# A two-layer attention kernel: new step order for the second layer, attention output normalised on VectorE

## What is computed

```python
# layer 0
x_norm = (x - mu) * rsqrt(var + EPS) * ln_scale + ln_bias
q, k, v = split(x_norm @ w_qkv + b_qkv)              # 8 heads of 16
attn = softmax(einsum('bqhd,bkhd->bhqk', q, k) * scale)
x = x + einsum('bhqk,bkhd->bqhd', attn, v) @ w_out + b_out
# layer 1
tokens = x @ Win + b_in
t = layernorm(tokens)
q, k, v = heads(t @ Wq), heads(t @ Wk), heads(t @ Wv)
pk, pv = pool2d(k), pool2d(v)                        # 64 positions
_, idx = top_k(einsum('bhsd,bhpd->bhsp', q, pk).max(axis=(1, 2)), 16)
attn = softmax(einsum('bhsd,bhkd->bhsk', q, pk[idx]) * scaling)
tokens = tokens + attn @ pv[idx]
ff = gelu(layernorm(tokens) @ Wf1 + bf1) @ Wf2 + bf2
out = (tokens + ff) @ Wout + bout
```

## Time and profile before

| | before |
|---|---|
| median of 3 runs | 921.74 us (920.42 to 923.03) |
| profiled execution | 920.22 us, its span 918.5 us |
| PE busy | 841.7 us, 92% |
| ACT busy | 615.3 us, 67% |
| DVE busy | 511.5 us, 56% |
| POOL busy | 162.5 us, 18% |
| mean granted TensorE clock | 0.961 |

### The profile page before, as it was taken

The page is one execution under the profiler, slowest core; times in us unless marked ns, Lnnn a source line. Parts: engine busy times, 40 slices in busy tenths (PEclk is TensorE's granted clock), DMA queues, the critical chain, the costliest instruction groups (busy, mean ns, idle before and its releaser), DMA issues.

```text
span 918.5 us, 14785 instructions
## 1 busy us (share of the span) xinstructions
PE 841.7 (92%) x5339; PEld 399.8 (44%) x5339; DVE 511.5 (56%) x1543; ACT 615.3 (67%) x699; POOL 162.5 (18%) x198
## 2 busy tenths in 40 slices
PE   8889989999898989999899988989899998899988
PEld 6324334444343433434344433444335343345665
DVE  6423267655577275754676365863666525633564
ACT  4577867587757867678666876578675876774112
POOL 2503041201330031300430022300412001000100
PEclk9799999999999999999999999999999999999979
DMA  3545324222331124322331123421142223000300
GB/s 72 98 74 94 60 47 88 39 35 59 93 64 33 26 48 105 53 36 59 75 65 29 32 59 92 70 36 38 28 89 45 36 59 69 1 1 25 70 0 25
DMA packets 41214, 48.73 MB, mean 53 GB/s; under 512 B 13872, under 2 KB 31920, under 8 KB 41136
## 3 DMA queue, kind: packets, MB, share of 16 engines
q1 hardware_dynamic: 41136, 47.72, 27.1%
HBM read 5.45 MB, written 4.19 MB: 10 GB/s over the span
## 4 chain that ended last, share of the span: by engine, by line
PE 60%; DVE 25%; ACT 8%; issue 3%; SPq 3%; POOL 1%; DMA 0%; DVEq 0%; ACTq 0%; POOLq 0%
PE O L545 17%; PE S L530 11%; ACT Pr L783 7%; DVE hT L1018 4%; PE BC L566 4%; PE BC L558 4%; PE BC L667 3%; PE BC L651 3%; PE A L477 3%; DVE st L893 3%; PE BC L588 2%; PE A L566 2%; PE S L763 2%; PE BC L606 2%; PE BC L659 2%
## 5 line engine op out<-in xcount | busy, mean ns | idle before, releaser
L783 ACT ACTIVATE Pr<-S 128x1024 f32<-128x1024 f32 x512 | 490.5, 1028 | 152.5 <-PE S L530 152.3
L545 PE MATMUL O<-Pr,Va 128*32 128x512 f32 x2048 | 279.3, 618 | 3.8 <-DVE Ot L997 3.8
L530 PE MATMUL S<-Qs,Ks 49*128 49x512 f32 x1024 | 213.3, 467 | 31.5 <-ACT Pr L783 28.8
L530 PEld LDWEIGHTS S<-Qs,Ks 49*128 49x128 f32 x1024 | 86.3, 186 | 160.8 <-ACT Pr L783 129.0
L545 PEld LDWEIGHTS O<-Pr,Va 128*32 128x32 f32 x2048 | 40.8, 108 | 87.3 <-issue 82.1
L383 POOL COPY Va<-v_new 128x256 f32<-128x256 f32 x32 | 12.4, 406 | 337.7 <-PE O L545 321.5
L799 ACT ACTIVATE tT<-BC,cols 128x512 f32<-128x512 f32 x32 | 24.1, 775 | 45.7 <-PE BC L558 45.7
L997 DVE COPY Ot<-O 128x512 f32<-128x512 f32 x32 | 21.9, 685 | 58.0 <-PE O L545 58.0
L1129 DVE TENSOR_SCALAR hT<-BC,cols 128x512 f32<-128x512 f32 x32 | 24.0, 751 | 45.4 <-PE BC L651 43.9
L1068 DVE TENSOR_REDUCE r<-BC 128x1 f32<-128x512 f32 x64 | 41.1, 681 | 12.9 <-PE BC L606 12.9
L1136 DVE TENSOR_TENSOR Y<-BC,out_bias 128x512 f32<-128x512 f32 x16 | 11.1, 691 | 61.5 <-PE BC L667 61.5
(11 more groups left out here) (190 smaller groups left out, 1149.2 us busy)
## 6 DMA issues: line engine op xcount, KB each, us to landing
Qs<-qh SPq DMA_DIRECT2D x128, 64.0 KB, 2.3
Ks<-kh SPq DMA_DIRECT2D x128, 64.0 KB, 2.3
Q1s<-q1h SPq DMA_DIRECT2D x64, 128.0 KB, 2.4
X<-in_x_dram SPq DMA_DIRECT2D x8, 512.0 KB, 4.0
Qs<-ql SPq DMA_DIRECT2D x64, 64.0 KB, 2.3
Ks<-kl SPq DMA_DIRECT2D x64, 64.0 KB, 2.3
Q1s<-q1l SPq DMA_DIRECT2D x32, 128.0 KB, 2.3
out_dram<-Y SPq DMA_DIRECT2D x16, 256.0 KB, 2.3
```

The lines of the kernel that those rows point to most:

```text
L530: mm = pe.matmul(S[:, c, a * HALF:(a + 1) * HALF], Ks[head, j, kb * P:(kb + 1) * P], Qs[head, j, c * HALF:(c + 1) * HALF], start=True, sto ...
L545: mm = pe.matmul(O[r:r + 32, :], Va[:, kb, 2 * j + a, :], Pr[:, s % 2, c, a * HALF:(a + 1) * HALF], start=(kb == 0), stop=(kb == TILES - 1))
L783: act.activation(Pr[:, s % 2, c, :], S[:, c, :], ACT.Exp, scale=SCALE).then_inc(probs_ready, 1)
```

## The change

- The AT_... constants are new. The second layer of an image now covers 46 steps: 32 beside the next image and 14 (`STEPS + s`: T2, FF, GELU, OUT) beside the image after that. TOKX of the next image moves across the border as well (steps 32 and 33), and the layer norm of X is done an image earlier (`first_norm`).
- Bank turns are worked out ahead of time in tables (`a_turns`, `b_turns`) instead of running counts.
- The attention output is no longer copied, turned by TensorE, divided, and turned back. VectorE transposes O in blocks of 32 x 32 into `OT`, divides there, transposes back into `On`, and four DMAs per pair write it into `attnT`.
- `Pr` has three buffers. TensorE adds one weighted sum in each step; that of step 31 stands at the end of its image, ahead of the next image's flag.
- The four matmuls of the sums of squares become one packed group (AT_BOUND, 26); one reduction over 128 rows, one transpose, and `bound` on one row replace four reductions.
- The product of tok2 with Wout is done in the OUT step, tok2T lies in Y, and `that` and `attnT` have tiles of their own.
- SP's list is reordered; in the tail it is: attention of pair 3, the store of image 6, the stack of image 7's queries, its store. The tail interleaves steps 32 to 45 of image 6 with steps 0 to 45 of image 7.

```diff
-AT_LN0, AT_XN, AT_Q, AT_K, AT_V, AT_TOKX = 2, (8, 10), (11, 12), (13, 14), (15, 16), (18, 19)
-AT_BOUND, AT_FLAG = (20, 21, 24, 26), 27
-AT_AT, AT_TOK, AT_T, AT_Q1, AT_PK, AT_SC, AT_RT, AT_RB = 2, 4, 7, 7, 9, (11, 12, 13, 14), 15, 16
-AT_SEL, AT_S2, AT_E2, AT_PT, AT_TOK2, AT_TT2, AT_T2 = 17, 18, 18, 20, 21, 23, 27
-AT_FF, AT_GELU, AT_OUT = (28, 29), 29, (30, 31)
-
+AT_LN0 = 22
+AT_XN, AT_Q, AT_K, AT_V, AT_TOKX = (10, 12), (15, 17), (19, 21), (23, 31), (32, 33)
+AT_BOUND, AT_FLAG = 26, 28
+AT_TOK, AT_T, AT_Q1, AT_PK, AT_SC, AT_RT, AT_RB = 3, 8, 9, 12, (15, 16, 17, 18), 19, 20
+AT_SEL, AT_S2, AT_E2, AT_PT, AT_TOK2, AT_TT2, AT_T2 = 22, 25, 25, 27, 29, 30, 34
+AT_FF, AT_GELU, AT_OUT = (37, 39), 41, (43, 45)
+AFTER_END = 46
 
...
-        Pr = sb("Pr", [P, 2, 2, T])
+        Pr = sb("Pr", [P, 3, 2, T])
...
+            def attn_out(n, j):
+
+                if j == 0 and n > 0:
+                    for h in range(2):
+                        sp.wait_ge(b_drained[h], b_after(n - 1, K_TOK + h))
+                sp.wait_ge(on_ready, PAIRS * n + j + 1)
+                for a in range(2):
+                    for c in range(2):
+                        r, d = 32 * (2 * a + c), HD * (2 * j + a)
+                        sp.dma_start(attnT[d:d + HD, c * HALF:(c + 1) * HALF], On[r:r + HD, j % 2, :]).then_inc(attn_in[j % 2], 16)
...
+            def image(n):
+
+                if n > 0:
+                    attn_out(n - 1, 3)
+                    stack(n, 2)
+                    stack(n, 3)
+                wait_for_flag(sp, n)
...
                     load_x(n + 2)
-                if not first:
+                attn_out(n, 0)
+                if n > 0:
                     stack1(n - 1)
...
+                if n > 1:
+                    store(n - 2)
+                attn_out(n, 1)
+                if n + 1 < IMAGES:
+                    stack(n + 1, 0)
+                attn_out(n, 2)
+                if n + 1 < IMAGES:
+                    stack(n + 1, 1)
+
...
+            attn_out(IMAGES - 1, 3)
+            store(IMAGES - 2)
...
+                if n == 0:
+                    normalise(1)
...
+            def sums_of_squares(bank, filled):
+
+                for i in range(2):
+                    for h in range(2):
+                        r = 32 * (2 * i + h)
+                        mm = pe.matmul(bank[r:r + 32, :], head_mask_b[:, :], squares[:, i, h * HALF:(h + 1) * HALF],
+                                       start=True, stop=True)
+                mm.then_inc(filled, 1)
...
                     scores(n, s, 1)
                     if s > 0:
                         weighted(n, s - 1)
-                    elif not first:
-                        weighted(n - 1, STEPS - 1)
-                    if s == 1 and not first:
-                        turn_o(n - 1, PAIRS - 1, turns)
-                    if s > 1 and s % TILES == 1:
-                        turn_o(n, s // TILES - 1, turns)
-                    if not last:
-                        before_tasks(n + 1, turns, s)
-                    if not first:
-                        after_tasks(n - 1, s, base + 1)
-
-            image(0, 0, first=True)
+                    if n > 0:
+                        before_tasks(n, STEPS + s)
+                    if n + 1 < IMAGES:
+                        before_tasks(n + 1, s)
+                    if n > 1:
+                        after_tasks(n - 2, STEPS + s)
+                    if n > 0:
+                        after_tasks(n - 1, s)
+                weighted(n, STEPS - 1)
+
+            image(0)
 
             pe.wait_ge(weights_in, 16 * WEIGHT_DMAS)
...
+            for s in range(AFTER_END):
                 for _ in range(WARM.get(s, 0)):
 
                     for a in range(2):
                         head = slice(64 * a, 64 * a + MROW + 1)
                         pe.matmul(S[:, 0, a * HALF:(a + 1) * HALF], Ks[head, 0, 0:P], Qs[head, 0, 0:HALF], start=True, stop=True)
-                after_tasks(IMAGES - 1, s, base + PAIRS + 1)
+                after_tasks(IMAGES - 2, STEPS + s)
+                after_tasks(IMAGES - 1, s)
...
+                g = STEPS * n + s
+                act.wait_ge(scores_ready, 2 * g + c + 1)
+                if c == 0 and g > 2:
+
+                    act.wait_ge(pv_done, g - 2)
+                act.activation(Pr[:, g % 3, c, :], S[:, c, :], ACT.Exp, scale=SCALE).then_inc(probs_ready, 1)
...
+                    if s == AT_TT2 and n > 0:
+                        act.wait_ge(out_done, 2 * 16 * n)
...
+            def bound(own, row):
+
+                both = prow[:, 0:P].rearrange("o (i h e) -> o i h e", i=2, h=2)
+                larger = prow[:, P:P + 64].rearrange("o (i e) -> o i e", i=2)
+                step(own, dve.tensor_copy(prow[:, 0:P], row))
+                step(own, dve.tensor_tensor(larger, both[:, :, 0, :], both[:, :, 1, :], ALU.max))
+                step(own, dve.tensor_tensor(prow[:, 192:224], prow[:, P:P + 32], prow[:, P + 32:P + 64], ALU.add))
+                step(own, dve.tensor_reduce(prow[:, 224:225], prow[:, 192:224], AX.X, ALU.max))
+                return dve.tensor_scalar(flag[:, :], prow[:, 224:225], SAFE_SQUARES, None, ALU.is_gt)
...
-            def copy_o(n, j):
-
+            def divide_o(n, j):
+
+                own = own_attention
+                if n > 0 or j > 0:
+                    dve.wait_ge(on_ready, PAIRS * n + j)
                 dve.wait_ge(pv_done, STEPS * n + TILES * (j + 1))
-                dve.tensor_copy(Ot[:, :], O[:, :]).then_inc(o_copied, 1)
-
-            def divide_o(n, j, turns, own):
-
-                drain_a(turns)
-                o = A[:, :].rearrange("p (t a c e) -> p t a c e", t=4, a=2, c=2)
-                r = rden[:, :].rearrange("p (t a c) -> p t a c", t=4, a=2)
-                step(own, dve.reciprocal(rden[:, :].rearrange("p (u o) -> p u o", o=1),
-                                        A[:, :].rearrange("p (u e) -> p u e", e=32)[:, :, HD:HD + 1]))
-                for c in range(2):
-                    ins = dve.tensor_tensor(
-                        attn[:, 4 * c:4 * c + 4, 2 * HD * j:2 * HD * (j + 1)].rearrange("p t (a d) -> p t a d", a=2),
-                        o[:, :, :, c, 0:HD], r[:, :, :, c:c + 1].to_broadcast([P, 4, 2, HD]), ALU.mult)
-                ins.then_inc(a_drained, 1)
+                dve.transpose(OT[:, :, :].rearrange("p q e -> p (q e)"), O[:, :]).then_inc(o_turned, 1)
+                dve.wait_ge(o_turned, PAIRS * n + j + 1)
+                step(own, dve.reciprocal(rden[:, :].unsqueeze(2), OT[:, :, HD:HD + 1]))
+                step(own, dve.tensor_tensor(OT[:, :, 0:HD], OT[:, :, 0:HD], rden[:, :].unsqueeze(2).to_broadcast([P, 16, HD]),
+                                            ALU.mult))
+                if n > 0 or j >= 2:
+                    dve.wait_ge(attn_in[j % 2], 16 * ATTN_DMAS * (PAIRS // 2 * n + j // 2))
+                dve.transpose(On[:, j % 2, :], OT[:, :, :].rearrange("p q e -> p (q e)")).then_inc(on_ready, 1)
...
-                    if s == 0 and not first:
-                        copy_o(n - 1, PAIRS - 1)
                     if s > 0 and s % TILES == 0:
-                        copy_o(n, s // TILES - 1)
-                    if s == 1 and not first:
-                        divide_o(n - 1, PAIRS - 1, turns, own_o)
-                    if s > 1 and s % TILES == 1:
-                        divide_o(n, s // TILES - 1, turns, own_o)
-                    if not last:
-                        before_tasks(n + 1, turns, own_b, s)
-                    if not first:
-                        after_tasks(n - 1, own_a, s)
-                assert last or own_b[2] == BEFORE_STEPS
-                assert first or own_a[2] == AFTER_STEPS
-
-            image(0, 0, first=True)
+                        divide_o(n, s // TILES - 1)
+                    if n > 0:
+                        before_tasks(n, STEPS + s)
+                    if n + 1 < IMAGES:
+                        before_tasks(n + 1, s)
+                    if n > 1:
+                        after_tasks(n - 2, STEPS + s)
+                    if n > 0:
+                        after_tasks(n - 1, s)
+                    if n == 0 and s == 0:
+                        first_norm(1)
+                    if s == AT_LN0 and n + 2 < IMAGES:
+                        first_norm(n + 2)
+                divide_o(n, PAIRS - 1)
```

More of the change, by code:

```diff
@@ L311, in _ @@
                 sp.dma_start(dst, src).then_inc(weights_in, 16)
-            def image(n, base, first=False, last=False, load=True):
-                wait_for_flag(sp, base)
+            def image(n):
[4 more added lines that the diff above has]
+                wait_for_flag(sp, n)
                 sp.sem_inc(sp_passed, 1)
@@ L522, in scores @@
                 before = 2 * STEPS * n + 2 * s + c - 1
[L523 removed]
+                if before > 0:
                     pe.wait_ge(probs_ready, before)
@@ L720, in _, with image @@
                 by_token_first(BC[h], xhT, win_s[:, :], h)
```

(20 more changed lines are left out.)

530 lines of the change are left out of this document (242 added, 288 removed).

## The result

The changed kernel takes 971.71 us (median of 4 runs, 968.29 to 972.49) where the kernel before takes 921.08 on the same chip (4 runs): 1.0548 times as long, 95% interval 1.0505 to 1.0591. The forecast was 945 with a range of 914 to 968, so the time lies 3.7 us outside the range. The direction was right, the size was 27 us short. The profiled execution took 972.3 with a span of 970.6, 26.8 over the 943.8 of the sum.

The account below looks back on a forecast made before the run. TensorE's in-order list was taken to bound the images, with 12% waits for other engines. 918.5 - 8 - 12.6 + 5 x 2.7 + 4.4 + 28 = 943.8, plus 1.7 around the span = 945.5, given as 945; range 914 to 968.

Parts of the forecast that it names:

- (a): Inner image, steps 9 to 11: exponential queued behind GELU, Q1 copies and table loads; TensorE waits plus half clock, 7.7 us.
- (b): Image border: TensorE waits for the last exponential, flag and branch, and TOKX tasks wait for V's drain and divide; 3.0 us.
- (e): Inner image, steps 15 to 18: waits around Q drains, score maxima and the second divide; 1.7 us.
- (c): Inner image, step 22: V's drain and third divide queue behind the layer norm on VectorE, sum 24 waits; 1.8 us.
- (d): Inner image, step 25: exponentials of the softmax of S2 sit ahead of the attention's exponential 26; 2.4 us.
- Image 0: Prologue and image 0: packed bound matmuls, TOKX gone, Q moved past a wait, border added; 8 us saved (5 to 10).
- Tail: After the last exponential: interleaving images 6 and 7 delays turned tokens, query stack and first scores; +28 us (+20 to +34).
- the rival of VectorE as the bound: Block transposes cost twice the copy, lengthening VectorE's waits by 3.5 us per inner image; 963 us, chance 0.13.
- only the first 0.7 holds up: VectorE's attention work, 2.3 us per pair: only the first 0.7 delays the next weighted sum, as the copy did.
- Table switches: Rival: ScalarE's table loads each cost a drain of 1.3 us, two loads in seven places, +18; 963 us, chance 0.03.
- The one that waits overlap: Rival: after (a) VectorE has caught up, so (c) to (e) and the half clock vanish; 902 us, chance 0.14.
- The one that inner images gain the removed work: Rival: inner images each gain 4.1 us, image 7 even, tail grows; about 907 to 925, centre 919, chance 0.11.

Follow-up runs that it names:

- standstill_filled_2: The changed kernel with 8 dummy matmuls ahead of the scores of step 11 in images 2 to 7; 957.34 us, ratio 1.0386.
- only_attention_part: The kernel before with only VectorE's block transposes, division and four DMAs per pair replacing the old attention output path, order untouched; 928.84 us, ratio 1.0053.
- three_repairs: The changed kernel with GELU in step 10, layer norm of X at step 12 (22 in image 0), image 6 finished before image 7 in the tail; 911.96 us.

## Why the prediction was right in direction and wrong in size

Of the 26.8 us missing, 14.4 lie in images 2 to 6, 6.2 in prologue and image 0, 3.6 in the tail, 1.8 in image 1, 1.0 in image 7 (27.0 with rounding).

The steps that failed are three terms of the sum. In an inner image the half clock was put at 1.7 us, behind one standstill only; it was 5.6. The work left on TensorE was put at 88.9; it was 92.0. In image 0 the forecast let a light step make up for a heavy one, which the trace doesn't bear out. The first two make 7.0 us an inner image; the forecast came within 2.9 of its length because the waits, 17.9 us in the forecast and 13.8 in the trace, were wrong the other way. That the sum is only 27 us off is in part luck. (The terms of image 7 in the prediction, 81.4 of work and waits of 20, make 101.4 and not 101.8; this changes nothing here.)

- **Wait (a), the standstill behind GELU: mechanism right, the half clock too small.** I had 5.5 + 0.5 of waiting and 1.7 of half clock. The waits were 4.72 and small ones; the half clock was 3.2 (standstill_filled_2). Together that is about 7.9 for the 7.7 of the forecast: the two errors cancel, and the 14.4 us come from elsewhere. I had scaled from one row of 3.4 us at half that follows a wait of 2.19; behind 4.7 the trace shows 6.8 and 10.2 us at half clock. A standstill twice as long brought two to three times as much.
- **Waits (b) to (e): the waits too large, the half clock left out.** I gave TensorE 17.9 us idle and it had 13.8. (c) came as walked (forecast 1.8 of waiting, 1.89 measured), with a norm of 5.9 for 4.8. (d) was 1.64 + 0.41 for 2.4. (b) was 0.38 + 0.78 + 1.67 at 535 to 541 us, 2.8 for 3.0. (e) was 0.6 by the idle times of steps 15 to 18 (0.95 in image 2), for 1.7. For the half clock behind (c) and (d) I had nothing; steps 25 to 28 carry 3.4 to 6.8 us of it in each image.
- **The work of an image: term mis-sized.** I had 93.0 before and 88.9 after; the traces give 95.4 and 92.0. Part of the 12.8 that I called waits was work. The saving is 3.4 for 4.1, in the division above. Which tasks make the 2.4 and the 3.1 us stays open: TensorE's busy time is modelled in part, and no run takes it apart.
- **Image 0: step failed.** The forecast was 8 us saved on prologue and image 0; it was 1.8 (107.8 to 106.0 in all). TensorE's idle time in image 0 rose from 5.3 to 8.5, though the wait of 3 for the stacks did go (step 12 fell from 5.09 to 2.92). I had let the steps with a task run at ScalarE's pace of 1.94, the light ones making up for the heavy (the prediction names that pace for image 1 only). The trace, TensorE and then ScalarE in steps 17 to 20 of image 0:

```profile
69.42 0.73 PE L587 MATMUL S<-Qs,Ks 49*128 49x512 f32 x4
70.08 1.07 PE L602 MATMUL O<-Pr,Va 128*32 128x512 f32 x8
71.08 0.50 PE L587 MATMUL S<-Qs,Ks 49*128 49x512 f32 x2
71.95 0.51 PE L587 MATMUL S<-Qs,Ks 49*128 49x512 f32 x2 [0.38 <-ACT Pr L812]
72.39 1.07 PE L602 MATMUL O<-Pr,Va 128*32 128x512 f32 x8
73.38 1.13 PE L540 MATMUL A<-xnT,wqkv_s 128*128 128x512 f32 x2
74.44 0.73 PE L587 MATMUL S<-Qs,Ks 49*128 49x512 f32 x4
```

```profile
69.96 3.77 ACT L812 ACTIVATE Pr<-S 128x1024 f32<-128x1024 f32 x4 [1.25 <-PE S L587]
74.98 3.77 ACT L812 ACTIVATE Pr<-S 128x1024 f32<-128x1024 f32 x4 [1.25 <-PE S L587]
```

  Two steps take 5.02, ScalarE works 3.77 of them and waits 1.25. S holds one step's scores, so TensorE can't run ahead in the light step; it waits there for the bank, then does sum and task, and ScalarE waits for it. That this is the whole of the 6.2 is read from the trace, not tried; steps 25 (4.84) and 31 (4.15) are the rest of it.
- **Tail: mechanism right, 3.6 short.** The marks behind the last exponential were 27.7, 47.7 and 57.9 for the turning of the tokens, the stack and the first scores; they came at 30.9, 53.3 and 62.7, and from there 47.3 for 47.6. What came late is the product of the tokens, 1.6 behind its old place as it waits for the attention DMAs, which the forecast left out, and work at half clock (16 passes 3.75 for 1.98, FF1 3.75). I had given that 0 to 3 in all; the tail has 34.6 us at half clock (14.0 before).
- **VectorE's attention part.** Transpose 0.711 for a forecast of 0.69, DMAs landing in 2.0 for 2.3; the tokens didn't wait for them in the inner images, but did in the tail, by 1.6 us in changed; I had named that as a sign of being wrong. The upper bound of twice the copy is out, and with it the rival of VectorE as the bound. The sentence quoted from the Trainium skill (Vector Engine (DVE) Microarchitecture Reference, 3.8) agrees with the measurement: the block transpose costs what the copy of the same tile does, 0.711 for 0.685. But that "only the first 0.7 holds up" was wrong: on VectorE itself the other 1.5 stood ahead of drains for which TensorE waits. only_attention_part lost by it what it had gained.
- **Table switches.** Between load and GELU there is 0.01 us (455.49 + 1.28 to 456.78), as in the trace of before; that rival is out.
- **Triple Pr** did nothing, as walked.
- **Rivals.** The one that waits overlap fell: (a) did not let (c) to (e) vanish. The one that inner images gain the removed work holds only where the standstills are repaired (three_repairs, 105.2; with the division split, 104.4).

## What to carry to other kernels

When steps are moved in an in-order list, price each standstill twice: once for the wait and once for the matmuls behind it at half clock, which here was 40% of the longest one's cost; over an inner image it was the largest term missing (5.6 us for 1.7). A task that switches ScalarE's table should not share a step with copies that stand ahead of the next exponential. If a wait can't be removed, useless matmuls placed inside it pay (14 us here, and a part of 13.7 in the tail), but they must stand where the bank is free, or they lengthen it.
